# Biased attention: a key tile's products in one block of 512 queries, in place of two blocks of 256

## What is computed

```
bias = m[:, None, None] * rel
score = jnp.einsum('bhsd,bhnd->bhsn', q, k) / scale + bias[None]
attn = jax.nn.softmax(score, axis=-1)
out = jnp.einsum('bhsn,bhnd->bhsd', attn, v)
```

## Time and profile before

| what | value |
|---|---|
| median of 3 runs | 5382.72 us (5376.99 to 5385.16) |
| span of the profiled execution, first to last instruction | 5239.6 us |
| PE, DVE, ACT, POOL busy | 4752.8, 4144.7, 3061.4, 1114.1 us |
| mean granted clock of TensorE | 0.954 |
| first to last score of the stage that is changed | 295.0 to 2951.3 us |

### The profile page before, as it was taken

How to read it: one execution, slowest core, us unless ns; L and a number is a source line. 1 busy time by engine, 2 the same in 40 slices (tenths; PEclk the granted TensorE clock), 3 DMA queues, 4 the chain that set the end, 5 groups by cost and what they waited for, 6 DMA issues and landing times. The chain is left out here.

```text
span 5239.6 us, 101423 instructions
## 1 busy us (share of the span) xinstructions
PE 4752.8 (91%) x39176; PEld 2431.7 (46%) x39176; DVE 4144.7 (79%) x5059; ACT 3061.4 (58%) x5260; POOL 1114.1 (21%) x1152
## 2 busy tenths in 40 slices
PE   6599999999999999999999888468899969999998
PEld 3233333333333333333333356335566646666666
DVE  4599999999999999999999233377765447888877
ACT  1168888888888887888888512112223225555553
POOL 0000012102121021220212110354320004344343
PEclk8689999999999999999999999789999979999999
DMA  5736635444443444444342137522110030110110
GB/s 183 173 87 147 135 63 124 73 81 82 74 90 64 84 79 82 74 74 79 68 85 48 36 116 235 187 89 73 57 52 5 3 131 24 30 29 25 30 29 17
DMA packets 242778, 421.67 MB, mean 80 GB/s; under 512 B 42569, under 2 KB 147034, under 8 KB 242256
## 3 DMA queue, kind: packets, MB, share of 16 engines
q1 hardware_dynamic: 195504, 341.87, 29.8%
q0 software_dynamic: 30048, 66.76, 4.1%
q10 hardware_dynamic: 16896, 8.39, 0.7%
HBM read 324.51 MB, written 129.17 MB: 87 GB/s over the span
## 5 line engine op out<-in xcount | busy, mean ns | idle before, releaser
L955 DVE TENSOR_REDUCE attn_mpart<-attn_ps_max 128x2 f32<-128x1024 f32 x2048 | 2473.0, 1224 | 66.8 <-PE attn_ps_max L1006 57.5
L820 ACT ACTIVATE attn_probs<-attn_ps_exp 128x512 f32<-128x512 f32 x4096 | 2231.0, 595 | 412.2 <-PE attn_ps_exp L1022 331.9
L1006 PE MATMUL attn_ps_max<-attn_keys,attn_quer 54*128 54x512 f32 x4096 | 1474.7, 461 | 88.5 <-DVE attn_mpart L955 54.5
L1022 PE MATMUL attn_ps_exp<-attn_quer,attn_keys 54*128 54x512 f32 x4096 | 1516.8, 448 | 0.2 <-ACT attn_probs L820 0.2
L1037 PE MATMUL attn_ps_out<-attn_probs,attn_vals 128*32 128x256 f32 x16384 | 1315.5, 393 | 9.8 <-ACT route_o L825 9.2
L1022 PEld LDWEIGHTS attn_ps_exp<-attn_quer,attn_keys 54*128 54x128 f32 x4096 | 620.8, 185 | 841.4 <-ACT attn_probs L820 775.7
L1037 PEld LDWEIGHTS attn_ps_out<-attn_probs,attn_vals 128*32 128x32 f32 x16384 | 324.0, 108 | 753.6 <-issue 422.4
L1006 PEld LDWEIGHTS attn_ps_max<-attn_keys,attn_quer 54*128 54x128 f32 x4096 | 588.7, 189 | 150.8 <-DVE attn_mpart L955 110.2
L1575 POOL DMA_INDIRECT ra_rows<-y_rows,slots x256 | 253.6, 990 | 324.7 <-DVE ra_total L1742 253.0
L577 POOL DMA_INDIRECT x_rows<-route_pay,route_now x256 | 251.6, 983 | 292.0 <-DMA x_rows<-route_pay,route_now 198.9
L1706 ACT ACTIVATE ra_row<-ra_psS 128x512 f32<-128x512 f32 x112 | 66.9, 597 | 372.2 <-PE ra_psS L1627 372.2
(11 more groups left out here) (367 smaller groups left out, 5396.9 us busy)
## 6 DMA issues: line engine op xcount, KB each, us to landing
attn_keys<-k_laid SPq DMA_DIRECT2D x256, 256.0 KB
attn_vals<-v_aug SPq DMA_DIRECT2D x128, 512.0 KB, 7.2
attn_keys<-k_laid SPq DMA_DIRECT2D x256, 128.0 KB
x_rows<-attn_zeros POOLq DMA_DIRECT2D x16, 1280.0 KB, 6.2
exp_x<-x_rows SPq DMA_DIRECT2D x64, 320.0 KB
exp_w1w<-in_w SPq DMA_DIRECT2D x64, 256.0 KB
y_rows<-exp_y SPq DMA_DIRECT2D x64, 256.0 KB
attn_keys<-k_laid SPq DMA_DIRECT2D x256, 48.0 KB
```

What stands on the lines that cost most here:

```text
L820: act.activation(probs[k % 2][:, j, :], ps_exp[bank_of(g, n)][:, :], ACT.Exp).then_inc(exp_done, 1)
L955: dve.tensor_reduce(mpart[i][:, kb, TC * pair + tile::TC * NPR], ps_max[buffer][:, :, :], AX, ALU.max).then_inc(unit_read, 1)
L1006: mm = pe.matmul(ps_max[buffer][:, h, :], quer[at % NG][half(h), pair, tile * P:(tile + 1) * P], keys[at % 2][half(h), pair, kb * CH:(kb + ...
L1022: pe.matmul(ps_exp[bank_of(g, n)][:, :], keys[g % 2][half(h), pair, k * P:(k + 1) * P], quer[g][half(h), pair, :], start=True, stop=True). ...
```

## The change

The four products of a tile are now issued once, each for all 512 queries, behind all four scores and both units of the next tile. There are 4 product matmuls per tile in place of 8; the sums are the same. `pv_done` now counts one block per tile, so all waits for it are halved. The buffers, the banks and the other waits stay.

```diff
-                def products(c, g, k, q):
+                def products(c, g, k):
 
                     s = NG * c + g
-                    if q == 0:
-                        pe.wait_ge(exp_done, EXPS * s + HG * (k + 1) + 2)
-                        if k % QUART == 0:
-                            pe.wait_ge(v_loaded[k // QUART], 16 * (s + 1))
-                        if k == 0:
-
-                            pe.wait_ge(o_copied, s)
-                    n = slice(q * CH // 2, (q + 1) * CH // 2)
+                    pe.wait_ge(exp_done, EXPS * s + HG * (k + 1) + 2)
+                    if k % QUART == 0:
+                        pe.wait_ge(v_loaded[k // QUART], 16 * (s + 1))
+                    if k == 0:
+
+                        pe.wait_ge(o_copied, s)
                     for j in range(HG):
-                        mm = pe.matmul(ps_out[j * VW:(j + 1) * VW, n], vals[:, k, j * VW:(j + 1) * VW],
-                                       probs[k % 2][:, j, n], start=(k == 0 and q == 0),
-                                       stop=(k == NT - 1 and q == 1), skip_group_check=True)
+                        mm = pe.matmul(ps_out[j * VW:(j + 1) * VW, :], vals[:, k, j * VW:(j + 1) * VW],
+                                       probs[k % 2][:, j, :], start=(k == 0), stop=(k == NT - 1), skip_group_check=True)
                     mm.then_inc(pv_done, 1)
...
-                        for q in range(2):
-                            for h in range(2):
-                                score(c, g, k, 2 * q + h)
-                                if ahead:
-                                    mm = unit_half(c, g, d, u + q, 1 - h)
-                            if ahead:
-                                mm.then_inc(unit_summed, 1)
-                            if k >= 1:
-                                products(c, g, k - 1, q)
-                            elif not first:
-                                products(*before, NT - 1, q)
+                        score(c, g, k, 0)
+                        if ahead:
+                            unit_half(c, g, d, u, 1)
+                        score(c, g, k, 1)
+                        if ahead:
+                            unit_half(c, g, d, u, 0).then_inc(unit_summed, 1)
+                        score(c, g, k, 2)
+                        if ahead:
+                            unit_half(c, g, d, u + 1, 1)
+                            unit_half(c, g, d, u + 1, 0).then_inc(unit_summed, 1)
+                        score(c, g, k, 3)
+                        if k >= 1:
+                            products(c, g, k - 1)
+                        elif not first:
+                            products(*before, NT - 1)
```

The waits on `pv_done` in `exps`, `copy_o` and SyncE's `step`, and its first increment, change from 2n to n:

```diff
-                    act.wait_ge(pv_done, 2 * (NT * s + k + 1))
+                    act.wait_ge(pv_done, NT * s + k + 1)
...
-                            hold(sp, pv_done, 2 * (NT * s + (b + 1) * QUART + 2), sp_passed)
+                            hold(sp, pv_done, NT * s + (b + 1) * QUART + 2, sp_passed)
```

More of the change, by code:

```diff
@@ L822, in copy_o @@
                 def copy_o(s, g):
-                    act.wait_ge(pv_done, 2 * (NT * (s + 1) + 2))
+                    act.wait_ge(pv_done, NT * (s + 1) + 2)
                     act.activation(r.o[g][:, :], ps_out[:, :], ACT.Copy).then_inc(o_copied, 1)
@@ L990, in _ @@
                 pe.sem_inc(unit_read, 2)
-                pe.sem_inc(pv_done, 4)
+                pe.sem_inc(pv_done, 2)
                 pe.sem_inc(exp_done, 2)
@@ L1103, in _ @@
                     step(NC - 1, g, left=min(2, NG - 1 - g))
-                for q in range(2):
-                    products(NC - 1, NG - 1, NT - 1, q)
+                products(NC - 1, NG - 1, NT - 1)
 def bias_constants():
```

## The result

The changed kernel is slower: 5513.7 us (4 runs, 5509.7 to 5517.4) against 5383.9 (4 runs, 5377.0 to 5390.9), a ratio of 1.0231 with a 95% interval of 1.0201 to 1.0261. Forecast were 5560 us in a range of 5485 to 5615, and slower with 94%. The time lies in the range, but not for the forecast's reasons alone: a term of 143 us that isn't there more than made up for 91 us of growth that the forecast missed (see the part on the prediction).

The account below looks back on a forecast made before the run. An undisturbed tile was taken as bound by PE (2.47 us), then DVE (2.26), then ACT. 212 for the longer round + 7 - 42 gave +177; span 5417 plus 143 made 5560 us, range 5485 to 5615.

Parts of the forecast that it names:

- a term of 143 us: Whole kernel: timed median taken to lie 143 us above the profile's span, untouched by the change, added to 5417.
- its pace behind the reciprocal: VectorE's reduces behind a long instruction, with units ready: 1.13 us apart against 1.23 otherwise, so 2.26 a tile.
- The new round: Undisturbed tile: score 3 waits for exponential 0, then the products block; 2.67 us against 2.47, +212 us over 1024 tiles.
- PE's share of the stage: Sign in the score stage's profile: TensorE's busy share was to fall from 98% to about 80%.
- TensorE's sum of 2.12: TensorE's own work per tile after the change, without waits for ScalarE: 2.12 us, 0.34 less than before.
- The narrow form of the rule on weight loads: Score pairs: each would pay its weight load, making TensorE's sum 2.34 us; relevant only if score 3's wait cost nothing.
- The disturbances: 131 us beyond undisturbed pace, from head-group boundaries and VectorE's other work: 42 us come back (10 to 110).
- The copy at the boundary: Head-group boundaries: the copy of ps_out stops holding back products; 31 x 0.36 = 11 us comes back.
- The last step: Last 32 tiles, without maxima: from 2.25 us a tile, not 2.47, so 7 us beyond the 212; nothing for the clock.
- The doubled block: Rival: wide passes hold each other up, products block costs 1.14 us, tile 2.82, total 5710 us; 7%.
- The free wait: Rival: score 3's wait costs nothing, TensorE's saving decides and VectorE binds at 2.26; 5200 us; faster, 4%.
- The 110 us of disturbances: Rival: the slower tile swallows most disturbances, 110 of 131 us come back, +109, total 5490 us; 11%.

Follow-up runs that it names:

- e4_prod256: Changed kernel with products of all but a step's first and last key tile on half the queries; span 5496.9 us, tile 2.26 at full clock.
- e1_nowait: Changed kernel without ScalarE's wait for the products of tile k-2 before a tile's first exponential; 5440.2 us, tile 2.61.
- e5_early512: Changed kernel with the 512-query products block moved between scores 1 and 2, last unit half behind score 3; 5505.5 us, tile 2.67.
- e9_short_first: Changed kernel with the first head's exponential on half its queries in 28 of 32 tiles; 5320.4 us, tile 2.45.
- e2_order: Changed kernel's order, all four scores first, but products as two blocks of 256 queries; 5538.2 us, tile 2.67.
- e0_before: The kernel before, unedited, profiled a second time; 5318.5 us, span 5316.9, tile 2.47.
- e7_filler: Changed kernel with four unread filler matmuls a tile where no units are left; 5462.5 us, last step's tile 2.66.
- e6_after: Changed kernel, unedited, run again beside the kernel before on another chip; 5498.8 us against 5334.0, ratio 1.0288.
- e8_threes: Kernel before with products blocks behind every third score, one group later, and three probs buffers; 5778.6 us, ratio 1.0805, tile 2.94.

## Why the prediction was right, point by point

**PE bound the tile before, and not DVE.** e4_prod256 reaches 2.26 at full clock with VectorE's work unchanged: VectorE could have been faster all along, as its pace behind the reciprocal said.

**The new round.** Right in each piece: score 3's load at 1.25 (forecast 1.24), the products at 1.67, the next tile at 2.67. The two passes of a block are 0.45 apart. The idle time is put down to ACT as forecast, and four edits (e1, e5, e9, e4) with four different predictions from the same pieces (2.61, 2.66, 2.47, 2.26) measured 2.61, 2.67, 2.45 and 2.26. A fifth didn't come out so: e2_order was forecast with 2.73 to 2.81 and measured 2.67, since its block was priced too high. In the first 31 steps the round gave 992 x 0.2015 = 200 us (forecast 205).

**The signs.** VectorE's gap is 0.31 (forecast 0.4). One sign failed: PE's share of the stage was to fall to about 80%, and it is 96% (a stretch of the changed kernel's profile, columns as in e0_before):

```profile
300.00:3050.00 2750.00, 2645.75 (x16145) 1042.13 (x16142) 2448.01 (x2518) 2078.91 (x4006) 422.48 (x465) 1.00 0.42 80
```

The 80% was TensorE's sum of 2.12 over 2.67, which counts the distance from start to start of a pair, 0.23. The profile's busy time counts each matmul for 0.39 to 0.50 us, and this covers most of the wait: the last unit half runs from 1651.98 to 1652.37, and score 3 starts at 1652.42. The wait is seen in the weight loads (0.48 idle at 1652.42) and in the distances, not in PE's share. And a tile without maxima is just as long as one with them only at full clock (2.67 in e5_early512, 2.66 with filler in e7_filler); in most of the last step it takes 4.13.

**PE's own work.** Scores 1 and 2 start 0.24 apart (forecast 0.23), behind a first distance of 0.34. The narrow form of the rule on weight loads (the Trainium skill, "TensorE: Matmul & The Clock Gate", Part 3) would have made it 0.34. The trace doesn't agree; the difference would have been hidden behind score 3's wait either way.

**The disturbances.** Forecast 42 us back. In the first 31 steps the excess over undisturbed tiles fell from 138 to 104 us, 34 back. Measured against e0_before, whose excess is 180, and e6_after's 101, it is 79, in part because that execution of the kernel before had 84 us of low clock in the stage. Executions of the kernel before differ by more than this term. By the first pair the disturbances shrank by a quarter, by the second by 44%, more than the third that the prediction named as a sign of being wrong; the pairs don't decide it. The copy at the boundary no longer holds up the products, as forecast: in 31 boundaries the first product starts 0.14 us behind the copy's end before, and 0.96 or more after.

**The last step.** Forecast +14 by the round (7 of the 212, and 7 more); the round gave 14 (2.67 x 32 = 85.4 against 71.3), and 42 more came from the clock (127.7 in all; in e6_after 32 more, 117.4 in all). Here the prediction's sentence failed that put nothing on the clock because a stretch without units had 1.00. That stretch had 2.25 us tiles; the changed one has the same work in 2.67, and there the clock fell to half. e7_filler shows that more work for TensorE keeps the clock. When it falls isn't worked out: 4, 23 and 66 us into the last step in three profiles with the same matmuls in 2.67 us tiles (the changed kernel, e6_after, e5_early512). In e9_short_first, where that step's tiles take 2.45, it didn't fall.

**What lies around the span.** The sentence that the timed median lies 143 us above the span, "which the change doesn't touch", was wrong: in every run that has both, the span is within 2 us of the time, and the profiled execution of before was an unusually short one. Profile to profile the attention's scores grew by 222 us: 200 by the round in 31 steps, 14 by the round and 42 by the clock in the last one, less 34. The forecast had 205 + 14 - 42 = 177. The rotary attention grew by 41 more, which isn't the change's, and the rest by 5. So the profiled span was forecast as 5417 and came out as 5508, 91 too low; the 143 us that aren't there were added, and 5560 lies 46 us above the median. That this was inside the range is in good part luck. So is the size of the change: +177 was forecast, and against the timed executions of before the loss is 130 (one chip) and 165 us (the other), against this profile of before it is 268.

Why the loss is smaller against the timed executions isn't shown, since none of some 5384 us was profiled. Ahead of the last step the changed kernel's two profiles have 14 and 19 us of low clock in the stage, those of the kernel before 36 and 84. That speaks for a slower tile that takes such stretches away, but e5_early512, with the same tile, has 63.

**The rivals.** The doubled block is out (the block takes 1.00 us, not 1.14). The free wait is out (score 3 waits in every tile of the changed kernel that is shown, and e1_nowait and e9_short_first move it). The 110 us of disturbances didn't vanish.

## What to carry to other kernels

Count the producers between two blocks against the buffers they go through: with n buffers, the (n+1)th in a row waits until the first one's consumer is done. Here a schedule that saved switches by making the runs longer than the buffers paid for that in every round, since nothing stood between the scores that could cover the wait. Sum the round from row to row, waits and signals with it; here such sums held to 0.02 us for the changed kernel and four of its edits, and missed where a price was guessed (e2_order) or a rhythm of the units wasn't thought through (e8_threes, by 0.6). The busy shares told nothing: before, TensorE and VectorE both had 98%, and after, TensorE has 96%. And check that a profile is an ordinary execution before its distance to the median is taken for a constant.

## What the runs showed of the hardware

- TensorE lost half its clock by being asked for less. In the changed kernel's last step it went from 1.00 to 0.50, 17 us after the last unit, and the filler's matmuls kept it at 1.00. In e4_prod256, where half the product columns were left out of nearly all tiles, it stood at 0.50 for 1338 of 2870 us, which took nearly all that the shorter work had gained. A TensorE that looks full can be at the low clock: between 2540 and 2600 us of that run PE was busy for 60.00 of 60 us at 0.50, and the clock rose only at 2602.
- Four passes of 256 columns on four column groups take 1.00 us to the next scores, as two of 512 do: within a block the width of a matmul is free. Two blocks of 256 with scores between them take 0.57 each, 1.14 together. I put the difference down to the change between the scores' weights (54 rows by 128 columns) and the products' (128 rows by 32, four times); no run separates it from the rest.
- The kernel before gave times from 5308 to 5391 us on the chips used, and one profile of 5240. Its longer executions had the lower mean granted clock: of the 11 on the second chip, the six up to 5334 us had 0.945 to 0.949, and the five from 5346 to 5382 us had 0.934 to 0.942. Low-clock stretches make part of the difference of the two profiles, about half of it in the attention by the estimate above. The rest isn't traced; ahead of one fall stand stops for which the profile shows no cause.
